# A graph attention block: segment search moved ahead of the projection, small transfers moved to ScalarE's queue, one load moved amid the edge loads

## The reference, cut to what matters

```
xn    = layernorm(x)                          # 6250 x 256
ft    = xn @ W_fc                             # 8 heads x 32
eh,et = <ft, attn_h>, <ft, attn_t>            # per node and head
ee    = <edge_attr @ W_e, attn_e>             # per edge and head, edge_attr 100000 x 64
e     = leaky_relu(eh[src] + ee + et[dst])
a     = softmax of e over the edges of one dst
```

## Time and profile before

| | |
|---|---|
| median of 3 runs | 3197.34 us (3195.78 to 3205.87) |
| profiled execution, its own time | 3193.17 us |
| its span, first to last instruction | 3191.5 us |
| TensorE busy | 2326.0 us, 73% |
| VectorE busy | 1756.4 us, 55% |
| ScalarE busy | 1318.4 us, 41% |
| GpSimd busy | 1840.9 us, 58% |
| the block that is changed | 2.5 to 323.2 us of the span |

### The profile page before, as it was taken

The page is one execution under the profiler, slowest core; times in us unless marked ns, Lnnn a source line. Parts: engine busy times, 40 slices in busy tenths (PEclk is TensorE's granted clock), DMA queues, the critical chain, the costliest instruction groups (busy, mean ns, idle before and its releaser), DMA issues. The chain is left out here.

```text
span 3191.5 us, 47998 instructions
## 1 busy us (share of the span) xinstructions
PE 2326.0 (73%) x11995; PEld 1945.7 (61%) x11995; DVE 1756.4 (55%) x5705; ACT 1318.4 (41%) x4659; POOL 1840.9 (58%) x1942
## 2 busy tenths in 40 slices
PE   4966576676766666588987888998788888645088
PEld 4865465666665655366775666776667666535077
DVE  5412888888888887566555333333333333366254
ACT  1532555555555445334554333333333332455033
POOL 1675777777777773220002777777777777250645
PEclk8988788888888787689998565556665565767589
DMA  6678444444444455710001333333333333311342
GB/s 194 171 174 243 113 114 111 112 113 111 111 112 112 111 132 135 249 39 22 14 27 59 106 106 105 105 105 106 106 106 105 105 105 105 114 55 36 99 145 84
DMA packets 266021, 349.56 MB, mean 110 GB/s; under 512 B 154605, under 2 KB 195475, under 8 KB 264245
## 3 DMA queue, kind: packets, MB, share of 16 engines
q0 software_dynamic: 89568, 235.89, 26.2%
q1 hardware_dynamic: 176190, 110.72, 13.6%
HBM read 289.49 MB, written 61.20 MB: 110 GB/s over the span
## 5 line engine op out<-in xcount | busy, mean ns | idle before, releaser
L1438 POOL DMA_INDIRECT Gb<-normed_rows,SRCT x784 | 741.2, 945 | 519.3 <-SPq L1430 280.8
L1459 PE MATMUL pAb<-HOTb,Gb 128*128 128x128 f32 x3136 | 847.8, 428 | 147.1 <-DMA Gb<-normed_rows,SRCT 114.1
L1459 PEld LDWEIGHTS pAb<-HOTb,Gb 128*128 128x128 f32 x3136 | 663.7, 298 | 331.2 <-DMA Gb<-normed_rows,SRCT 271.4
L1499 DVE TENSOR_TENSOR ACC<-ACC,pAb 128x256 f32 x784 | 330.7, 422 | 641.8 <-PE pAb L1459 568.7
L1029 POOL DMA_INDIRECT GX<-ft_rows,SRCT x432 | 412.1, 954 | 131.5 <-issue 129.1
L1118 ACT ACTIVATE ACC<-apA 128x254 f32 x784 | 300.4, 383 | 411.6 <-PE apA L1191 337.6
L1191 PE MATMUL apA<-AHOT,GX 128*128 128x129 f32 x1920 | 304.4, 329 | 84.0 <-DVE GX L1340 83.8
L1478 ACT ACTIVATE HOTb<-OFFb 128x1024 f32<-128x1024 f32 x98 | 103.6, 1057 | 604.8 <-PE pAb L1459 604.6
L1191 PEld LDWEIGHTS apA<-AHOT,GX 128*128 128x128 f32 x1920 | 290.1, 241 | 102.2 <-DVE GX L1340 102.2
L1029 POOL DMA_INDIRECT G<-ft_rows,SRCT x288 | 275.7, 957 | 87.6 <-issue 85.5
L1474 ACT ACTIVATE OFFb<-iota,NRELb 128x128 f32<-128x128 f32 x784 | 239.6, 388 | 6.7
(11 more groups left out here) (394 smaller groups left out, 3965.7 us busy)
## 6 DMA issues: line engine op xcount, KB each, us to landing
ebuf<-in_edge_attr_dram SPq DMA_DIRECT2D x49, 448.0 KB
Gb<-normed_rows,SRCT POOLq DMA_INDIRECT x784, 2.7
rows_by_expert<-ffn_PADT SPq DMA_DIRECT2D x1, 10360.0 KB, 41.6
sT<-rows_by_expert SPq DMA_DIRECT2D x80, 129.5 KB, 2.1
GX<-ft_rows,SRCT POOLq DMA_INDIRECT x480
sums_by_rank<-rrowa SPq DMA_DIRECT2D x49, 128.0 KB, 1.7
sums_by_rank<-rrowb SPq DMA_DIRECT2D x49, 128.0 KB, 1.7
GX<-in_x_dram SPq DMA_DIRECT2D x11, 560.0 KB
```

Source lines behind the costliest of these rows:

```text
L1438: pool.indirect_dma_start(G[g % R][m][:, :], None, TABLE[:, :], bass.IndirectOffsetOnAxis(ap=SRCT[:, t:t + 1], axis=0)).then_inc(g_in[g % ...
L1459: last = nc.tensor.matmul(pA[b][:, o:o + EP], G[k][m][:, c * 128:(c + 1) * 128], HOT[k % 2][:, m, :], start=True, stop=True)
L1499: last = nc.vector.tensor_tensor(acc[:, :, ds(b, EP)], acc[:, :, ds(b, EP)], pA[q][:, o:o + KD * EP].rearrange("p (c r) -> p c r", c=KD), ...
```

## The change

Five edits in `front`:

1. VectorE does all four batches of the segment search (bounds, hits, rows) around the first statistics and ahead of everything else; TensorE does its four batches ahead of its first turn. The transfer of dst that they need (DVI) is the first on SP's queue, and SNI is loaded from ScalarE's queue.
2. The flag transfers go to ScalarE's queue, issued after `keep(c)` of chunks 1, 4, 7 to 13 and 16 (`goes_on`), with their waits.
3. The rank transfers go to ScalarE's queue after chunks 9, 13 and 14 (`ranks`); the two NEXQ transfers change places.
4. SP loads F after the load of edge chunk 31, not after that of chunk 48.
5. TensorE's prefix matmuls are at chunks 4 and 6, its turning of the ranks at chunk 20.

```diff
@@ SP
+                for a in PARTS:
+                    sp.dma_start(DVI[a, :], ds32[a, :]).then_inc(dv_in, 16)
                 sp.dma_start(W[:, :, 0:D], W_fc.rearrange("(k p) n -> p k n", p=128)).then_inc(w_in, 16)
...
-                ds32 = dst.rearrange("(p j) -> p j", j=BK * BW)
-                for a in PARTS:
-                    sp.dma_start(DVI[a, :], ds32[a, :]).then_inc(dv_in, 16)
-                sp.wait_ge(idx_set, 1)
-                sp.dma_start(SNI[0:P - 1, :], ds32[1:P, 0:1], allow_slow_non_contiguous=True).then_inc(dv_in, 16)
...
                 load_x(1)
+                sp.wait_ge(idx_set, 1)
...
-                n = 4 * ER
-                for c in range(ER, n + 1):
+                for c in range(ER, LATE_F):
                     load(c)
-                sp.wait_ge(cont_ready, 1)
-                sp.dma_start(CONTD.rearrange("(p j) -> p j", j=ES), CONTB[:, :]).then_inc(cont_out, 16)
-                load(n + 1)
-                sp.wait_ge(rk_ready, 1)
...
-                for c in range(n + 3, NCH):
-                    load(c)
-
                 sp.wait_ge(rq_ready, 1)
                 sp.wait_ge(st, 16 * NT)
                 sp.dma_start(F[:, :], STARTD.rearrange("(p j) h -> p (j h)", j=ES)).then_inc(f_in, 16)
+                for c in range(LATE_F, NCH):
+                    load(c)
@@ PE
+                for b in range(len(SW)):
+                    segments(b)
                 pe.wait_ge(qf_ready, 1)
...
-                    if 1 <= g <= len(SW):
-                        segments(g - 1)
...
-                early, late = 3 * ER, 6 * ER
+                early, late = ER, 5 * ER
...
-                    if c == early + 1:
+                    if c == early + 2:
@@ ACT
+                def goes_on(c):
+                    if c == 1:
+                        act.wait_ge(cont_ready, 1)
+                        act.dma_start(CONTD.rearrange("(p j) -> p j", j=ES), CONTB[:, :]).then_inc(cont_out, 16)
+                    if c == 4:
+                        act.wait_ge(cont_out, 16)
+                        act.wait_ge(qf_ready, 1)
+                        act.dma_start(CONTQ, CONTD.rearrange("(b q p) -> q b p", q=QB, p=EP)).then_inc(cq_in, 16)
+                    if 0 <= c - 7 < QB // UT:
+                        u = c - 7
+                        act.wait_ge(cq_in, 16)
+                        cp = CONTP.rearrange("m (c j) -> m c j", j=EP)
+                        act.dma_start(cp[:, u:ES // UT:QB // UT, :], CONTQ[u * UT:(u + 1) * UT, :, :]).then_inc(cont_out, 16)
+                    if c == 16:
+                        act.wait_ge(cont_out, 16 + 16 * (QB // UT))
+                        act.dma_start(CONTU[:, 0:ES // UT * EP],
+                                      CONTP.unsqueeze(0).to_broadcast([H0, UT, ES // UT * EP])).then_inc(cu_in, 16)
+
+                def ranks(c):
+                    rq = RANKD.rearrange("(b q p) -> q b p", q=QB, p=EP)
+                    if c == 9:
+                        act.wait_ge(rk_ready, 1)
+                        act.dma_start(RANKD.rearrange("(p j) -> p j", j=ES), RK[:, :]).then_inc(rk_out, 16)
+                    if c == 13:
+                        act.wait_ge(rk_out, 16)
+                        act.dma_start(RQ[:, :, :], rq).then_inc(rq_in, 16)
+                        act.dma_start(BASEF[:, :], RANKD.rearrange("(o t p) -> o t p", o=1, p=EP)[:, :, 0],
+                                      allow_slow_non_contiguous=True).then_inc(rq_in, 16)
+                    if c == 14:
...
+                act.wait_ge(idx_set, 1)
+                act.dma_start(SNI[0:P - 1, :], ds32[1:P, 0:1], allow_slow_non_contiguous=True).then_inc(dv_in, 16)
                 root(0)
...
                     keep(c)
+                    goes_on(c)
+                    ranks(c)
@@ DVE
+                segment_bounds()
+                segment_hits(0)
+                segment_hits(1)
                 stats(0)
+                for b in range(len(SW)):
+                    segment_rows(b)
+                    if b + 2 < len(SW):
+                        segment_hits(b + 2)
...
-                segment_bounds()
-                segment_hits(0)
                 norm(1)
                 stats(1)
-                segment_hits(1)
...
-                    if 1 <= g <= len(SW):
-                        segment_rows(g - 1)
-                        if g + 1 < len(SW):
-                            segment_hits(g + 1)
```

More of the change, by code:

```diff
@@ L397, in front @@
         ftv = FT.rearrange("(p i) d -> p i d", i=NT)
+        ds32 = dst.rearrange("(p j) -> p j", j=BK * BW)
+        LATE_F = 8 * ER
         def chunk_of(g):
@@ L411, in _ @@
                 xv = x.rearrange("(p i) d -> p (i d)", i=NT)
-                rq = RANKD.rearrange("(b q p) -> q b p", q=QB, p=EP)
                 def load_x(q):
@@ L670, in rows @@
                     last.then_inc(row_ready, 1)
+                def goes_on(c):
[26 more added lines that the diff above has]
+                    if c == 14:
+                        act.dma_start(NEXQ[QB - 1:QB, 0:NQ - 1], rq[0:1, 1:NQ, 0],
+                                      allow_slow_non_contiguous=True).then_inc(rq_in, 16)
+                        act.dma_start(NEXQ[0:QB - 1, :], rq[1:QB, :, 0], allow_slow_non_contiguous=True).then_inc(rq_in, 16)
+                act.wait_ge(idx_set, 1)
+                act.dma_start(SNI[0:P - 1, :], ds32[1:P, 0:1], allow_slow_non_contiguous=True).then_inc(dv_in, 16)
                 root(0)
@@ L685, in _ @@
                     keep(c)
+                    goes_on(c)
+                    ranks(c)
             @block.vector
             def _(dve):
+                nc.vector.memset(SNI[:, :], 2 * N)
                 nc.vector.memset(DXI[:, 0:1], -1)
@@ L693, in _ @@
                 nc.vector.memset(QI[:, NQ - 1, :], 0)
-                nc.vector.memset(SNI[:, :], 2 * N)
                 dve.drain()
```

## The result

| | before | after | ratio, 95% interval |
|---|---|---|---|
| first measurement, median | 3196.56 us (3195.07 to 3205.87) | 3177.45 us (3172.31 to 3184.74) | 0.9934 [0.992, 0.9948] |
| again, on the chip of the runs below | 3200.54 us (3191.11 to 3206.35) | 3174.81 us (3172.78 to 3176.84) | 0.9918 [0.9904, 0.9931] |
| profiled execution, its own time | 3193.17 us | 3184.74 us | |
| profiled again | 3196.82 us | 3176.84 us | |
| barrier behind the block | 323.2, again 324.5 us | 300.1, again 299.1 us | |

The kernel is faster by 19 to 26 us, and the block by 23 to 25. I had forecast 29 for both, and a time of 3168 us: the sign and most of the mechanism were right, the size too large. Of the forecast's range, 3160 to 3177, the first median misses the upper end by 0.5 us; the second lies inside.

What follows compares the result with a forecast made beforehand. Bound: a serial end of edges, F, scans, sums and stores, plus a 27.5 us edge hole and GpSimd's late start. Edges to 288.0 plus 6 put the barrier 29 us earlier: 3193.17 - 29 = 3164, plus 4.2 gives 3168 us, range 3160 to 3177.

Steps and rivals of the forecast that it cites:

- Step 1: Search moved ahead on VectorE: search ends at 34 to 40, first scatter at 124.2 instead of 150.57, row gathers end at 269.6.
- The projection: TensorE and VectorE start it later, at 42 to 48: effect taken as 0, range -8 to +5.5 us.
- Step 3: F loaded amid the edges: holds them back 12 us, while scans and six of seven sums leave the end.
- the tail: Behind the edges, before the barrier: last sum, store and landing take 6 us, between 3.4 and 11.4.
- The sum: Whole block: first score at 121, edges paced to 288.0, 6 us behind them, barrier at 294, 29 us earlier.
- Step 2: Flags and ranks on ScalarE's queue: the 27.5 us hole on SP's goes, against 12 us of stalls, between 0 and 30.
- stall of 9 us: At edge chunk 20 TensorE waits for ranks: 5.2 us of remaining packets and 3.8 for VectorE.
- The check from the other side: Block's DMA total: queues busy 162 us between 118.5 and 323.2, so barrier not before 280.6, at most 42 us gained.
- The DMA bound from end to end: Whole block: ScalarE's transfers slip between edge packets, no stall seen, F's time covered; gain 41, 3156 us; chance 0.20.
- The hole that changes its place: ScalarE waits on its own transfers, TensorE stands 30 us at chunks 7, 13 to 20; gain 11, 3186 us; chance 0.12.
- Slower: ScalarE caught issuing BASEF, both NEXQ and CONTU, 15.5 us each; TensorE stands 62 us; 3218 us; chance 0.03.

Runs made afterwards that it cites:

- the first run: The changed kernel with only the search moved ahead, flag and rank transfers and F put back as before; 3203.67 us, 0.9987 of the kernel before.
- chunk 28: The changed kernel with TensorE's rank transposes before edge chunk 28 instead of 20; 3176.32 us, 0.9922 of the kernel before.
- the best: The changed kernel with rank transposes before edge chunk 28, NEXQ loaded over 112 partitions and CONTU in eight transfers; 3164.69 us, 0.9886 of the kernel before.
- these four: The changed kernel with later rank transposes, NEXQ over 112 partitions, CONTU in eight, or all three; 3733.12, 3731.95, 3730.7, 3732.0 us on the other chip.

## Why the prediction was right and where not

- **Step 1.** Right. The first gather at 35.0 (forecast 34 to 40), the first scatter at 122.6 (124.2), decided by the landing of ET as said. The projection was not 0 but at the good end of its bounds: ET stored 5.4 us earlier than in the earlier trace rows. It landed 6.4 us later, not the 2.4 of the earlier trace rows, with two edge chunks issued right behind it: the first scatter met its forecast because these two errors cancel. Row gathers ran from 187.4 (189.8) to 272.7 (269.6). That this alone pays little was in the argument ("GpSimd is no longer near the end") and is shown by the first run.
- **Step 3.** Right in its size: F in front of chunk 32 holds TensorE up by 12.3 us (12), the tail is 4.8 us from TensorE's end at 295.3 to the barrier (6), and the step is worth 12.
- **The sum.** TensorE ended 7.3 us later than the forecast 288.0. Its first score in the changed kernel, and the groups of scores in 118 to 189.8 and in 189.8 to 272.7:

```profile
115.35 1.95 PE L538 MATMUL pS<-VB,eT 128*128 128x128 f32 x16
```
```profile
L538 PE MATMUL pS<-VB,eT 128*128 128x128 f32 x323 | 41.4, 283 | 0.0
```
```profile
L538 PE MATMUL pS<-VB,eT 128*128 128x128 f32 x323 | 41.2, 282 | 0.0
```

At 16 a chunk these are 21.2 chunks by 189.8 (the first lies before 118) and 20.2 more by 272.7, where I had 21.3 and 20.8 by 269.6. From 115.35: 74.5 - 21.2 x 2.67 = 17.9 us beyond the pace, not 12. In the second stretch: 82.9 - 20.2 x 3.26 = 17.0, not 12. The last 7.6 chunks took 22.6 us, 2.3 more than at 2.67. That is 13.2 us too few, against 5.7 won by a first score at 115.35 in place of 121 and 1.2 in the tail: 6.3, about the 6.1 by which the barrier missed.
- **What the sum had at nothing.** It counts a stop by its wait alone. The waits of the first stretch were 11.1 us (7.5 for the ranks and 0.8 between their turns, 1.9 behind CONTU's issue, 0.9 for edges), close to the 12. The other 6 are work and clock: TensorE turns the ranks in 3.4 us without its waits, and behind the stop its granted clock is 0.50 until 188, which costs 2.4 us over the scores and the next turn. Behind F's stop it is 0.50 too, until 240, and the next chunk takes 5.2 us where 2.7 is usual, another 2.5 (1.0 and 2.1 in the profile taken again):

```profile
235.25 1.97 PE L529 MATMUL pE<-ident,ebuf 128*128 128x128 f32 x8 [12.32 <-DMA ebuf<-in_edge_attr_dram]
237.02 3.62 PE L538 MATMUL pS<-VB,eT 128*128 128x128 f32 x16
240.43 1.12 PE L529 MATMUL pE<-ident,ebuf 128*128 128x128 f32 x8
```

The rest of the second stretch, about 2 us, and the 2.3 behind it are small waits for edges.
- **Step 2, where the mechanism failed.** Its stall of 9 us was nearly right (7.5 measured), but by luck. I had the queue at 39 to 47 packets a us beside edges, and 5.2 us for what is left when TensorE stops, so the ranks would land at 179.6. The queue passed 1589 packets in 5 us beside the edges, far faster, and still the last rank landed at 176.5, since the last few hundred packets passed slowly. Nor was the stop what held the time, as chunk 28 shows. The sum has no term for DMA engines that stand unused while the ranks and CONTU move (busy 0.62 in 180 to 190 with chunk 28), and reshaping the two was worth 11.3 us at the barrier. (ScalarE got 15 issues, not 14, and the earlier trace rows has one of them, NEXQ's, at 4.71 us on SP; no sum rests on it.)
- **The check from the other side** (barrier not before 280.6) holds for every run on that chip, and the best comes within 7.2 us of it. It counts as full what all 16 engines can carry, so it bounds well only where the transfers spread.
- **Rivals.** The DMA bound from end to end (gain 41) fell in its form and survives in its idea: transfers, not ScalarE's waits, are the limit. The hole that changes its place (gain 11) fell: 13.5 us at chunk 20, not 30. Slower fell: ScalarE's longest issue was 3.70 us (4.06 in the second profile), with TensorE standing 1.9 on it. It was CONTU's, and the ranks in front of it made it long, not its own size: behind a reshaped NEXQ the whole CONTU was issued in 0.68 us, while behind the old one an eighth of it took 4.28.

## What to carry to other kernels

A wait removed is worth what is late next: a hole of 27.5 us went for 7, because the transfers that had made it now ran beside the edges, whose small waits grew by 9 us, and the ranks came 6 us late. Before moving a wait, look at the share of the DMA engines under it: with the transfer engines at 0.6 and a consumer waiting for data, a transfer's shape (a first dimension of 111, of 8) is the suspect: reshaping two transfers and moving the reader gained 11 us where moving the reader alone gained none. And a stop costs more than its wait: behind each of the two TensorE ran on at the lower clock, for 1.0 to 2.5 us more. Work moved off a chain pays only to the next chain's end (3.9 of 30 us here), so measure parts alone before adding them.

## What the runs showed of the hardware that was not expected

On the other chip the same program has its barrier at 460 to 469 us, not at 300. GpSimd issues its indirect transfers at the usual pace (one in 1.25 us), and meanwhile the other engines stop. VectorE's timeline there, in the kernel with chunk 28:

```profile
97.37 0.19 DVE L788 RECIPROCAL RSTD<-SDa 125x5 f32<-125x5 f32 x1 [45.06 <-issue]
```

GpSimd's gathers ended at 99.2. The DMA queues in 60 to 98, of that kernel there, and of the changed kernel on the first chip:

```profile
q0 software_dynamic: 1085, 0.56, 10.8%
q1 hardware_dynamic: 324, 0.56, 4.9%
```
```profile
q1 hardware_dynamic: 2408, 4.13, 34.2%
q0 software_dynamic: 1097, 0.57, 9.0%
q14 instruction: 3, 0.02, 0.2%
q8 instruction: 1, 0.02, 0.2%
```

As many packets of gathers, but none on the two queues that carry instructions, and 324 in place of 2408 on SP's, which issued 2 stores of rows there in place of 15. An engine whose next instructions are not yet there then stands until the gathers end ("issue": it waited for nothing that the profile shows). That the missing instructions are the cause is my reading of these rows, not tested; why this chip does it and the other not is open. The kernel before lost more there than these four, 51 to 53 us, but neither it nor the change itself was profiled there, so where that comes from is open too.
